# Prefix sums of 128 tokens each on TensorE, joined on VectorE by a column of the first half

## The reference

```
u  = layernorm(x)                                   # over the channels
K[c, t] = C[c] * A[c]**t * B[c],  A = sigmoid(A_param)
c  = causal_conv(u, K) + D * u                      # per channel, along the 256 tokens
y  = layernorm(u + gelu(c) @ W_proj.T + b_proj) * gamma + beta
x1 = x + layernorm(y)
v  = layernorm(x1);  v_prev = v shifted by one token
r  = sigmoid((mu_r*v + (1-mu_r)*v_prev) @ W_r.T);  k = relu((mu_k*v + (1-mu_k)*v_prev) @ W_k.T)**2
out = x1 + layernorm(r * (k @ W_v.T))
```

## Time and profile before

| | before |
|---|---|
| median of 3 runs | 165.47 us |
| the profiled execution | 164.04 us |
| its span, first to last instruction | 162.3 us |
| TensorE busy (matmuls) | 135.9 us, 84% |
| VectorE busy | 131.9 us, 81% |
| ScalarE busy | 134.3 us, 83% |
| GpSimd busy | 131.6 us, 81% |
| mean granted TensorE clock | 0.967 of full |

### The profile page before, as it was taken

The page is one execution under the profiler, slowest core; times in us unless marked ns, Lnnn a source line. Parts: engine busy times, 40 slices in busy tenths (PEclk is TensorE's granted clock), DMA queues, the critical chain, the costliest instruction groups (busy, mean ns, idle before and its releaser), DMA issues.

```text
span 162.3 us, 3207 instructions
## 1 busy us (share of the span) xinstructions
PE 135.9 (84%) x913; PEld 115.0 (71%) x913; DVE 131.9 (81%) x365; ACT 134.3 (83%) x395; POOL 131.6 (81%) x199
## 2 busy tenths in 40 slices
PE   0157895996899996999999999999999999999500
PEld 0055784895587966979879788799788778777500
DVE  0968999999999999999999989899998499730600
ACT  4357999878979895998999489989969979899970
POOL 4358899889898917498899979879988899989893
PEclk9999999599999999999999999999999999999965
DMA  3699900000000000000002020020402002222606
GB/s 103 153 272 330 275 2 2 4 0 2 0 0 4 0 0 2 6 0 0 0 0 69 0 65 2 4 69 0 129 0 69 0 0 67 69 65 65 194 1 193
DMA packets 18672, 8.98 MB, mean 55 GB/s; under 512 B 1504, under 2 KB 18656, under 8 KB 18656
## 3 DMA queue, kind: packets, MB, share of 16 engines
q1 hardware_dynamic: 18224, 8.79, 18.4%
q10 hardware_dynamic: 432, 0.00, 0.1%
HBM read 4.59 MB, written 4.19 MB: 54 GB/s over the span
## 4 chain that ended last, share of the span: by engine, by line
PE 62%; DVE 24%; POOL 5%; issue 3%; ACT 2%; ACTq 1%; POOLq 1%; DVEq 0%
PE ps_v L641 8%; PE ps_prefix L584 7%; PE ps_r L632 7%; PE ps_r L631 7%; PE ps_k L620 7%; PE ps_k L621 7%; PE ps_z L599 6%; DVE x_raw L391 4%; PE ps_prefix L586 4%; DVE ps_z L448 3%; PE ps_tT L611 3%; PE ps_xT L577 3%; DVE conv_scaled L426 3%; PE ps_z L600 3%; DVE conv L432 2%
## 5 line engine op out<-in xcount | busy, mean ns | idle before, releaser
L288 ACT ACTIVATE xn<-x_all,x_bias,x_r 128x128 f32<-128x128 f32 x64 | 26.2, 485 | 5.9 <-POOL x_bias L187 3.8
L344 ACT ACTIVATE f_normal<-f,out_bias,f_r 128x128 f32<-128x128 f32 x64 | 26.1, 485 | 1.5 <-POOL out_bias L237 1.5
L632 PE MATMUL ps_r<-mixed_T,tsT 128*128 128x128 f32 x128 | 24.7, 275 | 0.0
L631 PE MATMUL ps_r<-mixed_T,tsT 128*128 128x128 f32 x128 | 24.7, 275 | 0.0
L584 PE MATMUL ps_prefix<-prefix_ones,xn_pow 128*128 128x256 f32 x64 | 21.4, 418 | 3.8 <-DVE conv_scaled L426 3.6
L194 POOL TENSOR_TENSOR xn_pow<-xn,pow_token 128x512 f32<-128x512 f32 x16 | 20.3, 1271 | 2.4 <-ACT xn L288 2.4
L599 PE MATMUL ps_z<-pv_T,gelu 128*128 128x128 f32 x128 | 22.1, 277 | 0.0
L631 PEld LDWEIGHTS ps_r<-mixed_T,tsT 128*128 128x128 f32 x128 | 19.8, 192 | 2.4 <-issue 2.4
L249 POOL TENSOR_TENSOR x_all<-x_all,f_normal 128x512 f32<-128x512 f32 x16 | 20.1, 1273 | 0.0
L308 ACT ACTIVATE junk<-ps_z 128x128 f32<-128x128 f32 x64 | 16.8, 280 | 4.0 <-PE ps_z L600 3.7
L599 PEld LDWEIGHTS ps_z<-pv_T,gelu 128*128 128x128 f32 x128 | 19.5, 192 | 0.4 <-issue 0.4
(11 more groups left out here) (85 smaller groups left out, 347.5 us busy)
## 6 DMA issues: line engine op xcount, KB each, us to landing
out_x<-x_all SPq DMA_DIRECT2D x16, 256.0 KB, 2.2
x_all<-in_x SPq DMA_DIRECT2D x7, 512.0 KB, 5.9
x_all<-in_x SPq DMA_DIRECT2D x2, 256.0 KB, 3.6
w_pv<-in_W_proj SPq DMA_DIRECT2D x1, 64.0 KB, 4.6
w_pv<-in_W_v SPq DMA_DIRECT2D x1, 64.0 KB, 4.4
w_rk<-in_W_r SPq DMA_DIRECT2D x1, 64.0 KB, 5.0
w_rk<-in_W_k SPq DMA_DIRECT2D x1, 64.0 KB, 4.1
gamma_row<-in_gamma SPq DMA_DIRECT2D x1, 64.0 KB, 3.0
```

Source lines behind the costliest of these rows:

```text
L288: last = a_.activation(tile(xn[u % D], j), xa(u, j), ACT.Identity, bias=col(x_bias, u, j), scale=col(x_r, u, j))
L344: last = a_.activation(tile(f_normal[u % D], j), tile(f[u % D], j), ACT.Identity, bias=col(out_bias, u, j), scale=col(f_r, u, j))
L631: t_.matmul(tile(ps_r, j), tsT[u % D][:, q, l + 1:l + 1 + P], mixed_T[:, 0, :], start=True, stop=False)
L632: last = t_.matmul(tile(ps_r, j), tsT[u % D][:, q, l:l + P], mixed_T[:, 1, :], start=False, stop=True)
```

## The change

`prefix_sum` multiplies each of the four tiles with the 128 by 128 triangle alone, into its own 128 columns of `ps_prefix`. `convolve` scales the first tile of both sequences in one instruction of 128x256, and each second tile in one instruction of 128x128 that first adds a column, the last one of the first tile in `ps_prefix`, which holds that tile's total, and then multiplies. `prefix_ones` has 128 columns in place of 256. The calls themselves and their number are the same on every engine, but the written order on all four engines is another.

```
-        prefix_ones = sb("prefix_ones", SEQ)
+        prefix_ones = sb("prefix_ones", P)
...
@@ convolve(u) @@
-                v_.tensor_tensor(conv_scaled[u % D][:].rearrange("p (q l) -> p q l", l=SEQ),
-                                 ps_prefix[:].rearrange("p (q l) -> p q l", l=SEQ),
-                                 pow_down[:, None, :].to_broadcast([P, 2, SEQ]), ALU.mult).then_inc(scaled_ready, 1)
+                v_.tensor_tensor(conv_scaled[u % D][:].rearrange("p (q l) -> p q l", l=SEQ)[:, :, 0:P],
+                                 ps_prefix[:].rearrange("p (q l) -> p q l", l=SEQ)[:, :, 0:P],
+                                 pow_down[:, None, 0:P].to_broadcast([P, 2, P]), ALU.mult)
+                for j in range(1, TILES, 2):
+                    last = v_.scalar_tensor_tensor(tile(conv_scaled[u % D], j), tile(ps_prefix, j),
+                                                   ps_prefix[:, j * P - 1:j * P], pow_down[:, P:SEQ], ALU.add, ALU.mult)
+                last.then_inc(scaled_ready, 1)
...
@@ prefix_sum(u) @@
-                for q in range(2):
-                    t_.matmul(ps_prefix[:, q * SEQ:(q + 1) * SEQ], tile(xn_pow[u % D], 2 * q), prefix_ones[:],
-                              start=True, stop=False)
-                    last = t_.matmul(ps_prefix[:, q * SEQ + P:(q + 1) * SEQ], tile(xn_pow[u % D], 2 * q + 1),
-                                     prefix_ones[:, 0:P], start=False, stop=True)
+                for j in range(TILES):
+                    last = t_.matmul(tile(ps_prefix, j), tile(xn_pow[u % D], j), prefix_ones[:], start=True, stop=True)
...
@@ order on VectorE, from x_stats(10) to residual(7) @@
+            x_stats(10); t_stats_of(1); convolve(4); gamma_z(3); x_pooled(10, 2); scale_z(2); scale_z(3)
+            y_stats_of(2); y_stats_of(3); x_stats(12); convolve(5); residual(2); residual(3); t_stats_of(2)
+            x_stats(13); t_stats_of(3); convolve(6); x_stats(14); gamma_z(4); gate(0); gamma_z(5); scale_z(4)
+            scale_z(5); y_stats_of(4); y_stats_of(5); f_stats_of(0); convolve(7); residual(4); residual(5)
+            t_stats_of(4); t_stats_of(5); convolve(8); x_rsqrt(12, 4); gamma_z(6); gamma_z(7); scale_z(6)
+            scale_z(7); y_stats_of(6); y_stats_of(7); convolve(9); gate(1); residual(6); residual(7); f_stats_of(1)
+            convolve(10); t_stats_of(6); gamma_z(8); t_stats_of(7); gate(2); gamma_z(9); scale_z(8); scale_z(9)
...
@@ order on TensorE, from prefix_sum(8) to project(10) @@
+            prefix_sum(8); transpose_xn(8); project(6); keys(2); project(7); transpose_xn(9); values(1)
+            prefix_sum(9); gates(3); keys(3); transpose_t(4); gates(4); prefix_sum(10); transpose_xn(10); project(8)
+            project(9); prefix_sum(11); values(2); transpose_t(5); transpose_xn(11); keys(4); gates(5); values(3)
+            keys(5); values(4); prefix_sum(12); transpose_xn(12); project(10); transpose_t(6); project(11); keys(6)
...
@@ order on GpSimd, from t_scale_of(2, 2) to y_scale_of(6, 2) @@
+            xn_times_pow(6); xn_times_pow(7); x_scale_of(6, 10, 2); t_scale_of(2, 2); z_scale_of(4, 2)
+            scale_t_pool(3); xn_times_pow(8); xn_times_pow(9); y_scale_of(4, 2); f_scale_of(0, 1); add_f(0)
+            t_scale_of(4, 2); z_scale_of(6, 2); xn_times_pow(10); scale_t_pool(5); xn_times_pow(11)
+            y_scale_of(6, 2); xn_times_pow(12); xn_times_pow(13); f_scale_of(1, 1); z_scale_of(8, 2); add_f(1)
```

More of the change, by code:

```diff
@@ L252, in _ @@
             xn_times_pow(0); x_scale_of(1, 1, 1); x_scale_of(2, 2, 2); xn_times_pow(1); xn_times_pow(2)
[L253 to L266, removed]
+            x_scale_of(3, 4, 2); z_scale_of(0, 1); x_scale_of(4, 6, 2); xn_times_pow(3); z_scale_of(1, 1)
@@ L642, in values @@
                 last.then_inc(v_ready, 1)
-            transpose_xn(0); centre_bias(); prefix_sum(0); transpose_pv(); transpose_xn(1); prefix_sum(1)
-            project(0); transpose_rk(); transpose_xn(2); prefix_sum(2); project(1); transpose_xn(3); prefix_sum(3)
-            mix_weights(); prefix_sum(4); transpose_xn(4); project(2); project(3); transpose_xn(5); prefix_sum(5)
-            transpose_t(0); prefix_sum(6); transpose_xn(6); keys(0); gates(0); transpose_xn(7); prefix_sum(7)
-            transpose_t(1); project(4); project(5); keys(1); prefix_sum(8); transpose_xn(8); values(0)
@@ L649, in _ @@
-            transpose_t(2); gates(1); transpose_t(3); keys(2); gates(2); prefix_sum(9); transpose_xn(9); values(1)
-            project(6); project(7); gates(3); keys(3); transpose_xn(10); transpose_t(4); values(2); prefix_sum(10)
-            transpose_t(5); gates(4); keys(4); transpose_xn(11); project(8); project(9); prefix_sum(11); keys(5)
-            values(3); transpose_xn(12); gates(5); transpose_t(6); prefix_sum(12); transpose_t(7); keys(6)
-            values(4); project(10); project(11); transpose_xn(13); prefix_sum(13); keys(7); values(5)
@@ L654, in _ @@
-            transpose_t(8); gates(6); transpose_xn(14); transpose_t(9); keys(8); gates(7); values(6); project(12)
-            project(13); values(7); prefix_sum(14); gates(8); transpose_xn(15); keys(9); transpose_t(10); values(8)
-            prefix_sum(15); gates(9); values(9); keys(10); gates(10); project(14); transpose_t(11); project(15)
-            values(10); keys(11); transpose_t(12); gates(11); keys(12); values(11); transpose_t(13); gates(12)
-            keys(13); values(12); transpose_t(14); gates(13); values(13); transpose_t(15); keys(14); gates(14)
@@ L659, in _ @@
-            keys(15); values(14); gates(15); values(15)
+            transpose_xn(0); centre_bias(); prefix_sum(0); transpose_pv(); transpose_xn(1); transpose_rk()
+            prefix_sum(1); project(0); prefix_sum(2); project(1); transpose_xn(2); mix_weights(); transpose_xn(3)
+            prefix_sum(3); project(2); prefix_sum(4); transpose_xn(4); project(3); transpose_t(0); transpose_xn(5)
+            prefix_sum(5); keys(0); gates(0); transpose_t(1); transpose_xn(6); project(4); prefix_sum(6); project(5)
@@ new lines, in _ @@
+            transpose_t(7); gates(6); keys(7); values(5); transpose_t(8); transpose_xn(13); prefix_sum(13)
+            transpose_t(9); gates(7); prefix_sum(14); transpose_xn(14); values(6); project(12); project(13); keys(8)
+            values(7); gates(8); keys(9); transpose_xn(15); transpose_t(10); gates(9); values(8); keys(10)
+            project(14); prefix_sum(15); transpose_t(11); gates(10); values(9); project(15); values(10)
+            transpose_t(12); keys(11); gates(11); keys(12); transpose_t(13); gates(12); values(11); keys(13)
@@ L662 @@
+            values(12); transpose_t(14); gates(13); values(13); keys(14); transpose_t(15); gates(14); keys(15)
+            values(14); gates(15); values(15)
 _INS = ["x", "A_param", "B_vec", "C_vec", "D_vec", "W_proj", "b_proj", "gamma", "beta",
```

83 lines of the change are left out of this document (43 added, 40 removed).

## The result

| | before | after |
|---|---|---|
| median | 164.2 us (20 runs) | 165.91 us (20 runs) |
| ratio to before | | 1.0078, 95% interval 1.0057 to 1.0098 |

The forecast was 0.8 us faster; the kernel became 1.3 us slower (0.0078 x 164.2). Before took 164.2 us in the longer series, not the 165.47 us of its first three runs, so the comparison goes by the ratio. The ratio leaves out three disturbed executions of the changed kernel and lies at the ratio of the means (165.84 against 164.56), which is smaller than that of the medians, since six of the 20 times of before are 165 us and more and pull its mean above its median.

The account below looks back on a forecast made before the run. VectorE was taken to bound the early part, TensorE the late one, both nearly critical between. Three handovers near 150.2 plus 0.4 put the last `values` at 150.6, 0.8 earlier: 165.47 - 0.8 = 164.7 us, range 162.7 to 167.2.

Parts of the forecast that it names:

- TensorE's price: In `prefix_sum`, a unit takes 0.89 us for 1.31, a gain of 0.42; five units count, 2.10 us.
- VectorE's price: In `convolve`, scaling in three instructions for one costs 0.25 us more per unit, with 0 and 0.49 as bounds.
- The Newton steps: In `x_rsqrt` on VectorE, moved behind `convolve(8)`, two steps are no longer held by GpSimd's `xn_pow`: -1.87 us.
- The tail: On TensorE from `project(8)` to the last `values`: 74.2 us, each tail growing by 1.4 from the old queue of 72.8.
- the exchange itself is no gain: With holds left, VectorE's +2.5 us at `residual(7)` and the moved 3.5 us cost more than 2.1 us of matmuls return.
- first step: On VectorE ahead of `residual(6)`: same calls but two, 74.66 + 10 x 0.25 - 1.87 - 0.4 = 74.9 us.
- one new hold at half a chance: On VectorE at the `x_pooled` calls beside new neighbours: 0.5 us taken back from the 0.92 gained, net -0.4.
- second step: Handover from VectorE to TensorE: `residual(6)` first half done at 75.9 us, `project(8)` 0.1 later, then a 74.2 tail.
- The holds stay: Rival at VectorE's Newton steps: each remaining hold costs up to 0.97 us; time 165.7 with one, 166.6 with two; chance 0.20.
- Dear column: Rival in `convolve`: the column read from PSUM makes scaling +0.49 us per unit, time 166.8; chance 0.13.
- Half clock: Rival on TensorE: a 3 us stretch at 1.2 GHz ahead of a handover costs up to 1.5 us, 164.9 to 166; chance 0.06.
- Roots hold too: Rival at VectorE's Newton steps: two GpSimd roots hold them, 2.9 us not gained, time 167.6; chance 0.04.

Follow-up runs that it names:

- experiment 3: The kernel before in its old order, with the new `prefix_sum`, `convolve` and `prefix_ones` alone; ratio 1.0067 to before, 165.77 us.
- Experiment 2: The kernel before with the new order on all four engines, but the old prefix sum and scaling; ratio 1.0249 to before, 168.68 us.
- experiment 5: The changed kernel with the old 256-column prefix matmuls, overwriting, in units 0 and 1 alone; ratio 1.0135 to before, 166.55 us.
- experiment 8: The changed kernel with GpSimd's `xn_times_pow(3)` ahead of the root `x_scale_of(4, 6, 2)`, not behind it; ratio 1.0005 to before, 164.43 us.
- experiment 12: The changed kernel with VectorE's `x_pooled(8, 2)` moved behind `y_stats_of(0)` and `gamma_z(1)`, GpSimd's order unchanged; ratio 1.0042 to before, 165.23 us.
- experiment 6: The kernel before in its old order, with the new prefix sum and scaling for units 9 to 15 only; ratio 1.0005 to before, 164.01 us.
- experiment 10: The kernel before with `x_rsqrt(12, 4)`, `normalise(12)` and `normalise(13)` moved later, and the new form for units 9 to 15; ratio 0.9918 to before, 162.72 us.
- experiment 11: The kernel before with `x_rsqrt(12, 4)`, `normalise(12)` and `normalise(13)` moved later, and the new form for units 11 to 15; ratio 0.9937 to before, 162.91 us.
- experiment 4: The changed kernel with TensorE's 256-column prefix matmul back, the second tile's overwriting its half, VectorE's work unchanged; ratio 1.0273 to before, 169.06 us.
- experiment 7: The kernel before with `x_rsqrt(12, 4)` moved behind `convolve(8)`, and `normalise(12)` and `normalise(13)` behind `copy_xT(9)`; ratio 0.9933 to before, 163.03 us.
- experiment 1: The changed kernel run again without any edit, for a second trace; ratio 1.0084 to before, 166.03 us.

## Why the prediction was wrong

**Right.** TensorE's price: 0.89 a unit. VectorE's price: +0.25 a unit, the column from PSUM costing no more than one from SBUF (two instructions in 0.61, rows above). The Newton steps: free, and by more than 1.87, since `x_rsqrt` from `x_neg` to `x_bias` fell by 2.6, from 4.99 to 2.40. The tail: 74.39 for 74.2. The statement that the exchange itself is no gain: experiment 3.

**Wrong, first step: "Ahead of `residual(6)` the new order has the same VectorE calls", 74.66 + 2.5 - 1.87 - 0.4 = 74.9.** Measured 76.82. The same calls took the same time, but the waits between them were counted as those of before. VectorE's idle time from 13 us to `residual(6)` is 0.38 + 0.74 + 1.11 + 0.24 + 0.33 + 0.28 = 3.08, against 0.55 + 0.23 + 0.28 = 1.06: +2.0. The forecast's "one new hold at half a chance", 0.5, was a whole one of 1.10, and the old one of 0.92 went: +0.18 for the forecast's -0.4, or 0.6 lost. The Newton steps gave 0.7 more. 74.9 + 2.0 + 0.6 - 0.7 = 76.8. Experiment 2 shows that it was the order and not the form: with the old form it is 4.3 late by the same sum. Where the +2.0 comes from is shown only in part: 0.9 of it, the wait at `gamma_z(0)`, falls away when the matmuls are fast early (experiment 5), but other waits are new in that trace, whose clock fell later on, so that no single cause is shown for it.

**Wrong, second step: the handover "`residual(6)` -> `project(8)`: 75.9 + 0.1".** It was not a handover in the new order. TensorE started `project(8)` 2.13 after `residual(6)`, not 1.1, because `gates(3)` and `gates(4)` had waited 0.65 and 1.32 for ScalarE's `tanh`. The forecast had summed TensorE's calls behind the handover and none of those ahead of it, though they too had been put in a new order, as had ScalarE's. The real handover is `residual(4)` -> `project(6)`, from where the chain goes over ScalarE's squares and `tanh` to `gates(4)` and `project(8)`. In both traces of the changed kernel and in experiments 5, 8 and 12, whose `residual(4)` lies between 60.09 and 62.76, `residual(4)` to `project(8)` is 17.45 each time. The first half of `residual(6)` is done about 1.0 us ahead of `project(8)`. So `residual(6)` is late for a cause that it shares with `project(8)`: all six waits and the new hold lie at or ahead of `residual(4)`, and what is lost by then reaches the last `values` undiminished (experiments 8 and 12: 1.41 and 0.74 at `residual(4)` and at the end). The Newton steps, on which the forecast's gain rested, lie behind `residual(4)` in the new order and not on the chain. What they would have added there, had they been held, no run shows.

By places, the two misses, 1.9 and 1.0, and 0.2 in the tail, less the 0.4 held in reserve, make 2.7: 150.6 became 153.34. By cause this sum is not to be read as two independent losses.

**The rivals.** The holds stay: no, those of the Newton steps went, but a hold of the same kind appeared at another place, `x_pooled(8, 2)`. Dear column: no. Half clock: in part open. Slow matmuls up to 18 or 21 us occur in every trace with the new form in units 0 and 1, and two traces put them at some 0.9 us (experiment 5). The first trace, with a granted clock of 0.50 from 27.9 us on, has its last `values` 1.27 later than the second, but the second has none of it and is 1.93 late all the same. Before has such a stretch too, from about 28.8 to 32.2 us. Roots hold too: no; the 128x16 instructions of 0.17 at 68.06 and 69.33 read two SBUF tensors and lie within GpSimd's roots at 67.06 and 69.07. By the rule of the Trainium skill (SBUF — State Buffer, Who interferes with whom) they would have been held; the measurement decides. (The row at 21.41, which the prediction set against this rule, has one tensor as input, and so is not the case of two that the prediction stated.)

**What the forecast did not ask: who is next behind TensorE.** It let TensorE's saved time count in full behind the handover. In the old order it does not: experiments 6, 10 and 11 take 2.1 to 2.9 us from TensorE and the median falls by 0.3 at most, as GpSimd's roots and additions come up beside it. The new order has 3.5 us more of TensorE's calls behind `project(8)`. That this is why TensorE stays the bound there, and why the saving counts there (experiment 4, 1.89 us of tail), is argued from the sum and not shown by a run of its own.

## What to carry over

Where all engines run in orders written by hand, price a reordering by the queues on both sides of a handover, and count the waits in the stretch before it as part of the cost. They are not a constant that carries over from the old trace. Follow the chain back from the handover before you price it: here it left VectorE at `residual(4)` and not at `residual(6)`. A short VectorE instruction beside GpSimd's `xn_pow`, 1.26 us long over two SBUF tensors, lost up to 1.1, so look for every such pair in the new order before counting on one that goes. And before a saving on the bounding engine is counted, look at how full the next engine is: here 2.9 us of saved matmuls brought 0.3 at most.

## What was not expected of the hardware

The moment at which TensorE's matmuls become fast differs between executions of the same instructions. In experiment 7 it came after `prefix_sum(1)`, in experiment 11, the same code up to there, before it; the granted clock reads 1.00 in both. The first matmuls of `prefix_sum(1)` in the one and the other:

```profile
16.76 1.06 PE L584 MATMUL ps_prefix<-prefix_ones,xn_pow 128*128 128x256 f32 x2
17.62 0.63 PE L586 MATMUL ps_prefix<-prefix_ones,xn_pow 128*128 128x128 f32 x2
```

```profile
16.24 0.70 PE L594 MATMUL ps_prefix<-prefix_ones,xn_pow 128*128 128x256 f32 x2
16.77 0.38 PE L596 MATMUL ps_prefix<-prefix_ones,xn_pow 128*128 128x128 f32 x2
```

VectorE's scaling waits for it, 0.88 against no wait, `residual(0)` is 1.0 us apart (30.82 and 29.83), and so is `residual(6)` (76.99 and 75.97). A single trace of this kernel can thus mislead by 1 us on the time of a landmark, as much as the effects sought here; lengths between landmarks of one trace (the tail is 74.39 in experiments 1, 5, 8 and 12, which have the calls of the changed kernel behind `project(8)`) are far steadier.
